# A two-stream expert kernel: the second expert layer as three fp16 products, all expert weights kept on the chip, later normed rows by ScalarE

## The reference, cut to what matters

```python
# round 0:  x = x + 0.5 * moe0(norm(x))            24 experts, hidden 512, the top 2 of each token
# round 1:  x = x + linear_attention(norm(x)); x = x + 0.5 * moe0(norm(x))
# round 2:  x = x + 0.5 * (shared(norm(x)) + moe1(norm(x)))      8 experts, hidden 256, top 2
# round 3:  x = x + causal_attention(norm(x)); then as round 2
def body(acc, expert):
    w1e, b1e, w2e, b2e, ce = expert
    h = jax.nn.gelu(xf @ w1e + b1e, approximate=False)
    y = h @ w2e + b2e
    return (acc + ce[:, None] * y, None)
```

## Time and profile before

| | |
|---|---|
| median of 3 runs | 1047.45 us |
| lowest and highest run | 1044.62 us, 1049.02 us |
| span of the profiled execution | 1043.2 us |
| TensorE busy | 905.4 us (87%) |
| VectorE busy | 569.7 us (55%) |
| ScalarE busy | 484.6 us (46%) |
| GpSimd busy | 497.2 us (48%) |
| moved by DMA | 200.19 MB, 192 GB/s |

### The profile page before, as it was taken

One profiled execution on the slowest core, in us unless ns is written; L12 is line 12 of the kernel. 1 busy time (PEld: TensorE's weight loads), 2 busy tenths in 40 slices (PEclk: granted clock), 3 DMA queues, 4 the chain that ended last, 5 costly groups with the idle time before them and its releaser, 6 DMA issues.

```text
span 1043.2 us, 26677 instructions
## 1 busy us (share of the span) xinstructions
PE 905.4 (87%) x8696; PEld 789.0 (76%) x8696; DVE 569.7 (55%) x2226; ACT 484.6 (46%) x814; POOL 497.2 (48%) x519
## 2 busy tenths in 40 slices
PE   4757999998999799999999998996899999998670
PEld 2327899976889777899888898883688867888570
DVE  7897500066785065785058400588883888872112
ACT  3333544448634257734345444352528455654320
POOL 0551560271027571035372743577744657277655
PEclk9886999999999899999999999898999999999985
DMA  9765999973578783488895899944658456669982
GB/s 306 242 205 156 300 308 242 237 203 95 123 191 231 187 212 104 118 208 234 218 254 146 209 274 226 230 129 130 153 141 189 124 115 165 142 155 247 258 196 75
DMA packets 278655, 200.19 MB, mean 192 GB/s; under 512 B 146112, under 2 KB 233536, under 8 KB 278400
## 3 DMA queue, kind: packets, MB, share of 16 engines
q1 hardware_dynamic: 262144, 164.90, 63.1%
q0 software_dynamic: 16384, 33.59, 11.2%
HBM read 115.56 MB, written 55.57 MB: 164 GB/s over the span
## 4 chain that ended last, share of the span: by engine, by line
PE 58%; DVE 20%; DMA 8%; issue 5%; ACT 4%; POOL 4%; SPq 1%; DVEq 0%; POOLq 0%; ACTq 0%
PE bank L1425 20%; PE bank L1403 5%; PE bank L1405 5%; PE bank L1404 5%; DMA turned<-rows 4%; PE bank L1291 4%; POOL got L2123 3%; PE bank L1244 3%; DMA got<-y_l,slot_index 3%; PE bank L1263 2%; PE bank L1220 2%; PE bank L1253 2%; PE bank L1422 2%; DVE xn L1708 2%; PE bank L1301 2%
## 5 line engine op out<-in xcount | busy, mean ns | idle before, releaser
L1425 PE MATMUL bank<-second,hid 128*128 128x128 f32 x2560 | 369.7, 287 | 0.0
L2123 POOL DMA_INDIRECT got<-y_l,slot_index x256 | 244.7, 956 | 236.4 <-DMA y_l<-y 114.3
L1425 PEld LDWEIGHTS bank<-second,hid 128*128 128x128 f32 x2560 | 324.7, 195 | 4.7 <-issue 3.0
L2103 POOL DMA_INDIRECT rows<-rows_sent,slot_index x192 | 187.8, 978 | 282.2 <-issue 167.7
L1575 ACT ACTIVATE hid<-bank 128x512 f32<-128x512 f32 x320 | 189.7, 597 | 280.4 <-PE bank L1405 266.0
L1403 PE MATMUL bank<-turned,blocks_l 128*128 128x128 f16 x1280 | 239.7, 222 | 41.1 <-DMA turned<-rows 31.2
L1921 DVE SCALAR_TENSOR_TENSOR x_res<-got,share,x_res 128x128 f32<-128x128 f32 x256 | 77.4, 348 | 319.5 <-DMA got<-y_l,slot_index 312.9
L1405 PE MATMUL bank<-turned,blocks_l 128*128 128x128 f16 x1280 | 239.8, 223 | 0.0
L1404 PE MATMUL bank<-turned,blocks_l 128*128 128x128 f16 x1280 | 239.1, 222 | 0.0
L1403 PEld LDWEIGHTS bank<-turned,blocks_l 128*128 x1280 | 127.6, 100 | 55.4 <-issue 52.7
L1404 PEld LDWEIGHTS bank<-turned,blocks_l 128*128 x1280 | 127.1, 99 | 8.9 <-issue 5.9
(11 more groups left out here) (208 smaller groups left out, 1215.6 us busy)
## 6 DMA issues: line engine op xcount, KB each, us to landing
second<-in_w_dram SPq DMA_DIRECT2D x243, 256.0 KB, 5.3
y_l<-y SPq DMA_DIRECT2D x104, 256.0 KB
second<-in_w_dram SPq DMA_DIRECT2D x192, 128.0 KB
got<-y_l,slot_index POOLq DMA_INDIRECT x256
rows<-set SPq DMA_DIRECT2D x1, 3584.0 KB, 14.9
rows<-set SPq DMA_DIRECT2D x7, 512.0 KB, 6.4
rows<-rows_sent,slot_index POOLq DMA_INDIRECT x192
hid<-in_w_dram SPq DMA_DIRECT2D x9, 256.0 KB, 5.2
```

The costliest lines, as they stand in the source:

```text
L1425: m = t.do.matmul(out, hid[:, at], second[:, at], start=False, stop=(c == C - 1))
L2103: d = g.do.indirect_dma_start(rows_dram[s], at, rows[:, 2 * D * i:2 * D * i + 2 * D], None)
L2123: d = g.do.indirect_dma_start(got_mem[slot][:, col:col + D], None, y_dram[layer][s][layer.team(ev.i)], at)
```

## The change

1. **Second layer.** h x w2 becomes three fp16 products, as in the first layer. ScalarE writes the gelu back into the bank, then writes its high half (times 16) as fp16 to SBUF. VectorE subtracts to get the low half. TensorE runs 12 fp16 matmuls a unit in place of 4 fp32 ones. The output is scaled back in `copy_y`.
2. **All weights stay.** w2 of every expert is loaded once at the start, and cut into halves: ScalarE makes the high half, TensorE subtracts it (an fp32 identity matmul and an fp16 one, 512 columns), and ScalarE makes the low half. 28 such parts. `bring_second` and SyncE's reading of expert numbers go.
3. **Room for it.** The 128-column selectors become one column that is read 128 times. `blocks_l1` (2.1 MB) is parked in HBM once made and brought back after the last linear attention; two sets lie over it meanwhile. A third set is its own. The tables of the causal attention are loaded late, over `blocks_l0`. `rows_sent` has six buffers. Four buffers for raw weights are those of `got`, four those of `hid`.
4. **Norm.** From round 1 on, VectorE writes only minus mean times root, and ScalarE writes the normed rows (four operations of 128 x 128 with scale and bias from SBUF).
5. **Empty tiles.** 55 tiles are computed of 56, and 23 of 24. That leaves 316 units, eight of which have one tile.
6. **Order.** First-layer units may be three ahead, `hid` has four buffers. The first layer's bank is held until VectorE has made the low half. Planned durations and priorities are new.

```diff
-        self.units = self.tiles // self.unit
+        self.bound, self.unit = bound, SEQ // hidden
+        self.units = -(-bound // self.unit)
...
-RAW_BUFFERS = 10
+GOT_BUFFERS, HID_BUFFERS, ROW_BUFFERS = 4, 4, 6
+RAW_BUFFERS = [HID_BUFFERS + GOT_BUFFERS, GOT_BUFFERS]
...
-        "bring": [[(SY, 0.45 * unit + 0.08, 0.0), (DMA, 0.9, 2.0)]],
...
+        "l1": [[(PE, 0.68, 0.22), (SC, 0.58, 0.16)]], "hid": [[(SC, 0.6, 0.16), (VE, 0.7, 0.1)]],
+        "l2": [[(PE, 0.75 if unit == 1 else 0.8, 0.22)]], "ystore": [[(SC, 0.55, 0.15)] + copied(256)],
...
+        yield from load("park")
+        for n in PARKED_SETS:
+            self.open_set(n)
...
+        yield Await(["linears"])
+        self.grow(self.mid_sets, MID_SETS, Ev("linears", 0, 0, 0))
+        yield from load("unpark")
...
+            yield Take(self.hid, [l1], 1)
+            yield from self.stage("hid", s, p, unit, {VE: lambda: self.give(self.banks, (l1, 0))})
+            yield Await([("l1", s, p, min(unit + FIRSTS_AHEAD, units[-1]))])
...
+            def second_left(ev, layer):
...
+                t.do.matmul(bk[:, :], ccol("ident"), raw, start=True, stop=False)
+                t.wait_ge(*w2_high.after(Ev("upper" + ev.kind[5:], *ev[1:])))
+                m = t.do.matmul(of_unit(bk[:, :], layer), minus, part_of(layer, ev, 2), start=False, stop=True)
...
-                    for c in range(C):
-                        at = slice(j * H + c * P, j * H + c * P + P)
-                        m = t.do.matmul(out, hid[:, at], second[:, at], start=False, stop=(c == C - 1))
+                    _, _, high, low, select = block_parts(block_for(ev, j), H)
+                    t.do.matmul(out, spread(select), bcol("b2_0" if layer is L0 else "b2_1"), start=True, stop=False)
+                    for c, at in enumerate(spans(C)):
+                        upper = hid[:, j * H + c * P:j * H + c * P + P]
+                        t.do.matmul(out, upper, high[:, at], start=False, stop=False)
+                        t.do.matmul(out, upper, low[:, at], start=False, stop=False)
+                    t.wait_ge(*hidden_low[ev.s].after(Ev("hid", *ev[1:])))
+                    for c, at in enumerate(spans(C)):
+                        lower = hid[:, SEQ + j * H + c * P:SEQ + j * H + c * P + P]
+                        m = t.do.matmul(out, lower, high[:, at], start=False, stop=(c == C - 1))
...
+            def place_norm(ev):
...
+                for i in range(BT):
+                    root, minus_mean = sm[:, 2 * BT + i:2 * BT + i + 1], sm[:, 3 * BT + i:3 * BT + i + 1]
+                    m = a.do.activation(xn[:, D * i:D * i + D], x[:, BT * ev.i + i, :], ACT.Identity, bias=minus_mean, scale=root)
...
-                m = a.do.activation(hid, hb[:, :], ACT.Gelu, scale=1 / (X_SCALE * W_SCALE))
-                m.then_inc(hidden_gelu[ev.s].sem, 1)
+                a.do.activation(hb, hb, ACT.Gelu, scale=1 / (X_SCALE * W_SCALE)).then_inc(hidden_gelu[ev.s].sem, 1)
...
+                m = a.do.activation(hid[:, 0:n], bank_of(l1)[:, 0:n], ACT.Copy, scale=HID_SCALE)
...
+            def low_hidden(ev):
...
+                v.wait_ge(*hidden_high[ev.s].after(ev))
+                m = v.do.scalar_tensor_tensor(hid[:, SEQ:SEQ + n], bank_of(l1)[:, 0:n], HID_SCALE, hid[:, 0:n], ALU.mult, ALU.subtract)
...
+            def park_blocks(ev):
+                y.wait_ge(*w1_low.after_all(w1_splits[1]))
+                y.wait_ge(*w2_low.after_all(w2_halves[1]))
+                y.wait_ge(*selects_made.after(SELECTS))
+                y.do.dma_start(blocks_dram, blocks[L1][:, :]).then_inc(block_parked.sem, 16)
...
-            def bring_second(ev, expert):
```

More of the change, by code:

```diff
@@ L73 @@
 L1 = Layer("l1", 8, 256, 2)
+assert all(l.teams == 1 or l.units * l.unit == l.tiles for l in (L0, L1))
 MAX_TILES = max(l.tiles * l.teams for l in (L0, L1))
@@ L466, in prepare @@
             self.spawn(load("load_x", 0, b), rank)
-        for kind in ("load_half", "load_bias", "load_cut"):
+        for kind in ("load_half", "load_bias"):
             self.spawn(load(kind), rank)
+        self.spawn(selects(), rank)
+        self.spawn(ready(), rank)
         yield Sleep(4.0)
-        parts = [part(n) for n in range(len(W1_PARTS))]
-        for n, steps in enumerate(parts):
-            self.spawn(steps, (0, 2, n))
+        parts, later = W1_PARTS[0] + W2_PARTS[0], W1_PARTS[1] + W2_PARTS[1]
+        for n, ev in enumerate(parts):
+            self.spawn(first(ev) if ev.kind.startswith("w1") else second(ev), (0, 2, n))
             if n == 3:
@@ L678, in experts @@
         rank, turn = (2 * p + s, 3, team), Ev("experts", s, p, team)
-        left = {g: per_group for g in layer.rows(team)}
+        left = {g: sum(unit // per_group == g for unit in units) for g in layer.rows(team)}
         def fetch(g):
@@ L1418, in layer2 @@
+                hid, ob = hid_mem[plan.hid.at[l1]].bitcast(F16), bank_of(group)
+                t.wait_ge(*selects_made.after(SELECTS))
+                t.wait_ge(*bias_split.after(BIAS_DONE))
+                if layer is L0:
+                    t.wait_ge(*w2_low.after_all(w2_halves[0]))
+                else:
+                    t.wait_ge(block_back, 16)
+                t.wait_ge(*hidden_high[ev.s].after(Ev("hid", *ev[1:])))
                 bank_free(group)
-                for j in range(layer.unit):
+                for j in range(layer.filled(ev.i)):
@@ new lines, in load_raw @@
+            def load_raw(ev, layer, source):
+                raw, loaded = raw_of(ev)
+                old = plan.raw[int(ev.kind[3:])].before[ev]
+                if old:
+                    y.wait_ge(*(w1_part if old.kind.startswith("w1") else w2_left).after(split_of(old)))
+                elif layer is L1:
+                    y.wait_ge(*w1_low.after_all(w1_splits[0]))
+                    y.wait_ge(*w2_low.after_all(w2_halves[0]))
+                src = source[ev.i * layer.unit:(ev.i + 1) * layer.unit].rearrange("e d h -> d e h")
+                y.do.dma_start(of_unit(raw, layer), src).then_inc(loaded.sem, 16)
```

614 lines of the change are left out of this document (358 added, 256 removed).

## The result

The changed kernel takes 1175.69 us (median of 4 runs, 1173.17 to 1176.8) against 1048.05 us before (median of 4, the three of before and one more): a ratio of 1.122 (95% interval 1.117 to 1.127). It is 12% slower where 8% faster was forecast. The profiled execution has a span of 1175.5 us.

The account below looks back on a forecast made before the run. It took TensorE alone to bound dense stages, and TensorE and VectorE both nearly full to bound mixed ones. Terms -85 - 12 + 17 - 20 + 13 = -87 us took 1047.45 us to 960 us; range 915 to 1010 us.

Parts of the forecast that it names:

- the term of -85 us: Second layer on TensorE: twelve fp16 matmuls for four fp32 save 0.27 us a unit over 316 units, 85 us.
- The sum: Whole kernel: all terms together take 87 us off the median, from 1047.45 to 960 us.
- -85 - 12 + 30: TensorE's work: second layer saves 85 us, tiles left out save 12, cutting 28 parts of w2 adds 30.
- rival B: Mixed stages keep their old pace because ScalarE has no room: 42 of the 85 us go, about 1002 us; chance 0.16.
- Tiles left out: Expert rounds: four whole units and eight half units fewer, together 12 us saved.
- Cutting w2: Start and first dense stage: TensorE's cutting of w2 into halves, partly covered by idle time, adds 17 us.
- DMA: Transfers and SyncE: fewer bytes and shorter waits take 20 us off the 83 us of DMA on the chain.
- ScalarE and VectorE: Added hidden layer steps and moved norms: 768 us busy on ScalarE, 735 on VectorE, costing 13 us.
- the +13 us: Cost taken for three hand-over steps on two engines, a bank held longer and copies before attention steps.
- A: DMA waits worth more: 40 us off the chain, ScalarE and VectorE cost nothing, 927 us; chance 0.12.
- C: VectorE's low halves stand behind 32 adds waiting for gathers, stopping TensorE: 145 us lost, 1092 us; chance 0.08.
- D: Dense stages don't quicken, since bank gelu or stationary loads cost what is saved: 1045 us; chance 0.04.

Follow-up runs that it names:

- e4: Changed kernel with both layers and the selector reading the first expert's block at fixed addresses: 1208.32 us, ratio 1.022.
- r1: Changed kernel as it is, run again on another chip: 1302.43 us, ratio 1.106 to the kernel before there.
- e7: Changed kernel with all addresses fixed and the hidden layer's halves left out on ScalarE and VectorE: 1027.77 us, ratio 0.981.
- e8: Changed kernel with its register addresses kept and the hidden layer's halves left out on ScalarE and VectorE: 1181.45 us, ratio 1.128.
- v1: Kernel before with w2 cast once to fp16 and brought to a fixed address, low halves of w2 and hidden layer left out: 1011.67 us, ratio 0.966.
- r2: Kernel before as it is, run again on the chip of r1: 1175.09 us.
- e13: e4 again, on one chip with e14: 1204.06 us, ratio 1.019 to the kernel before.
- e14: e7 again, on one chip with e13: 1196.07 us, ratio 1.011 to the kernel before.
- e3: Changed kernel with all twelve second layer matmuls of a tile reading one 128-column piece at the tile's register address: 1235.35 us, ratio 1.042.

## Why the prediction failed

**The second layer: the term of -85 us.** This is the step that failed: the second layer's twelve matmuls were priced at 0.67 us, and the instructions between them at nothing. I took 0.67 us for twelve fp16 matmuls from the earlier trace rows and carried it over to twelve others. Those rows were first layer matmuls that followed four fp32 ones of 0.235 us each. In the record of that unit TensorE's sequencer has worked five of its nine addresses out during the fp32 matmuls (161.49 to 162.09 us), ahead of their use, and the other four during the first layer. The first layer's pace was held only with the help of the fp32 matmuls that the change takes away, and the change adds eight addresses at the same time. Per unit of the 24-expert layer: 2.26 us of sequencer over 1.40 us of array, where it was 9 x 0.14 = 1.3 us under 1.67. The term came out as +0.59 us a unit in the dense stages in place of -0.27. 316 units at 0.59 would be +186 us; the mixed stages, where TensorE waits for others anyway, took less, and e4 against r1, each beside the kernel before on its own chip, gives about 99 us for all addresses, e7 against e8 154 us. The trace of before held the hint: the page says that register instructions aren't counted as busy, and the block's address was worked out per tile. I asked what a matmul costs and not what stands between two. The Trainium skill (Trainium Architecture — The Big Picture, Inside one NeuronCore) says that each engine has its own instruction stream with one sequencer; e8's row agrees, with 315 matmuls in 30 us while every other engine had time.

**The sum.** Even with all addresses fixed, and 1.40 us a unit as forecast, e4 is at 1.02 and not 0.92. I counted a microsecond off TensorE as one off the span, at 87% busy. The runs say otherwise. On the chip where the kernel before takes 1047 us, e7 has TensorE busy for 838.0 us, 67 less than before, which is what the forecast's terms for TensorE come to (-85 - 12 + 30), and gains 19; v1 has 750.5 (155 less) and gains 35. TensorE's idle time grows instead, from 138 to 189 and 261 us of the span. Where it grows differs by run. In e4 against r2, both on chips where the kernel before takes some 1180 us, the waits for ScalarE grow from 26.5 to 77.5 us and the idle time without a cause from 75 to 127, while the waits for fetched rows fall from 26.1 to 2.7. In e7 against the kernel before, the waits for ScalarE grow from 16 to 57 us and those for fetched rows from 31.2 to 73.6. One row of each, TensorE's waits (total, times, longest), for e4, before and e7:

```profile
PE bank L1352 <- ACT xn L1654: 27.8, 9, 12.2
...
PE bank L1403 <- DMA turned<-rows: 31.2, 10, 6.8
...
PE bank L1550 <- DMA turned<-rows: 73.6, 9, 24.7
```

The forecast also has no term for the clock. With more idle time TensorE was at its lower level for longer: the mean granted clock is 0.889 in e4 against 0.924 in r2, which is 269 against 180 us at 1.2 GHz, and 0.916 in e7 and 0.893 in v1 against 0.954 before (175, 219 and 98 us). TensorE was busy for 183 us of e4's low time and 118 of r2's. If half of that is lost, since matmuls start 0.11 us apart there and not 0.056, the clock took back some 32 us in e4 (an estimate from these rows) and, in the same way, some 17 us in e7 (85 against 51 us busy at the low level). No run holds the clock fixed, so this isn't shown by an experiment.

In e7 three of the waits for fetched rows make 57 us, the longest while GpSimd issues a round's scatters. GpSimd and the first matmul after, e7:

```profile
321.80 0.96 POOL L2311 DMA_INDIRECT rows<-rows_sent,slot_index  x1 [5.71 <-DVE slot_index L2049]
323.13 0.97 POOL L2311 DMA_INDIRECT rows<-rows_sent,slot_index  x1 [0.37 <-issue]
324.40 0.96 POOL L2311 DMA_INDIRECT rows<-rows_sent,slot_index  x1 [0.30 <-issue]
...
347.74 0.26 PE L1550 MATMUL bank<-turned,blocks_l 128*128 128x128 f16 x1 [24.66 <-DMA turned<-rows]
```

16 scatters at 1.26 us (0.96 and a gap of 0.30 for which the profile names no cause) are 20 us, and behind them the fetch. 512 such gathers and scatters are 645 us of GpSimd's list, though the page of each kernel calls GpSimd busy for less than half of the span. In the kernel before the longest wait of TensorE for fetched rows was 6.8 us, and in e4 1.9 us: this hand-over from round to round holds e7 up, not the changed kernel with its steps. There rival B is nearer, with more waiting for ScalarE and less for VectorE (54 us in r2, 44 in e4).

**Tiles left out** were there: 404 bias matmuls in place of 416. **Cutting w2**: the first `layer2` came at 103.1 us, just past my 95 to 103 and 8.6 us after the 94.5 of the kernel before, where 8 were forecast as not covered, and TensorE had 76.52 of the first 100 us. **DMA**: 126.35 MB moved, 128 forecast. The chain has 1% of DMA where it had 8%. The first row, of the profile of after, adds up to 61% only, since that chain reaches back only to about 460 us; the second is r1's, the same kernel, and whole:

```profile
PE 44%; DVE 8%; ACT 3%; issue 3%; POOL 2%; DMA 1%; POOLq 0%; ACTq 0%; DVEq 0%
...
PE 67%; DVE 9%; issue 9%; ACT 9%; another core or an unknown queue 3%; DMA 1%; POOL 1%; SPq 0%; ACTq 0%; DVEq 0%
```

r2, the kernel before on r1's chip, has 3% of DMA, with 5% under "another core or an unknown queue". So much of it came off, and brought nothing, since TensorE's pace took its place. **ScalarE and VectorE**: 725.9 and 724.7 us against 768 and 735 (735 is 77% of the forecast time, not within the "80 to 87%" that the prediction gives for all three engines). A norm step on ScalarE takes 0.484 us, not 0.37. That is nearer to the 0.46, an estimate with the 93 ns for a pointer operand of the Trainium skill (ScalarE: Activation LUTs, What ACT_TABLE_LOAD costs), so there the page was the better source than a row of another form. Whether the +13 us that I took for the place of these steps is right isn't shown: e13 and e14 differ by 0.9 points, some 10 us, but also in the order of the work.

**The rivals.** A is out by its sign. C's total was the nearest, 1092 against 1176, for a wrong reason: its stops would be idle time of TensorE behind an add that waits for `got`, and that wait fell from 312.9 to 45.7 us, with TensorE idle for 37 us in all on VectorE. B's mechanism shows once the addresses are fixed (e4), but doesn't make the kernel slower than before. D is nearest to the truth: the dense stages didn't quicken. But I gave it 0.04, and bounded it at "what is saved is lost", although nothing kept the period from rising. The uncertainty that I never priced was an operation that the profile's views don't list. The range should have had one more rival: more instructions a unit on TensorE, priced by the span between matmuls.

## What to carry to other kernels

When matmuls get shorter, count the instructions between them, not the matmuls alone. An operand at a register's address has its price for each new address, here 0.13 to 0.14 us, which 0.056 us matmuls don't hide; four fp32 ones of 0.235 us a unit helped to hide nine of them, but not thirteen. Bring what a register chooses into a buffer at a fixed address, or let several matmuls use one address. A busy share that is made of modelled durations can stand at 98% while the engine does half of what it could, so compare counts a microsecond. And before a saving on the fullest engine is taken whole, look for the next in line at each change of stage: here 67 us less of TensorE were worth 19 us (e7). Where idle time grows, look at the granted clock as well.

## What the runs showed of the hardware

- An address instruction on TensorE costs 0.13 to 0.14 us of its sequencer, by the periods of 2.26 and 1.71 us with 17 and 13 of them; in the record of after they mostly follow each other at 0.124 us. A matmul whose address is known costs it close to nothing: 25 of them went at 1.40 us with ten address instructions beside.
- A moving operand at a register's address is read as fast as one at a fixed address (e3: 0.056 us apart).
- Sets on different chips differ by up to 13% on one and the same kernel (1047 and 1183 us). Part of it is idle time of TensorE with no cause in the trace, in gaps of mostly 0.3 to 0.5 and 1.0 to 1.2 us. The kernel after has 18.2 us of it in one profile and 84 us in the one on another chip. Another part is the granted clock (0.954 and 0.924 for the kernel before).
- Behind such gaps, 1.10 and 1.06 us long, TensorE's granted clock was 0.50 from 361 to 364 us of e4, and its matmuls started 0.11 us apart, not 0.056.
- A ratio moves by a point or two between chips, so a pair that has to be told apart within that belongs on one chip.
